# Perceiver layer on one core: P times V per head on four column groups, the mask added by TensorE, minima of two score banks at a time

## What is computed

```python
qh = split_heads(layernorm(x) @ Wq + bq)             # (64, 16, 32, 32)
kh, vh = split_heads(ctx @ Wk + bk), split_heads(ctx @ Wv + bv)   # (64, 16, 257, 32)
logits = einsum('bhqd,bhkd->bhqk', qh, kh) / sqrt(32)
logits = logits + mask * -1e9                        # mask: one row of 257 per sequence
attn = softmax(logits)
out = einsum('bhqk,bhkd->bhqd', attn, vh)
x = x + out.transpose(...).reshape(...) @ Wo + bo
```

## Time and profile before

| | us |
|---|---|
| median of 3 runs | 2039.79 |
| lowest and highest of them | 2039.04, 2040.78 |
| the profiled execution | 2034.94 |
| its span, first to last instruction | 2033.2 |
| TensorE matmul busy in it | 1902.7 (94%) |
| TensorE weight load busy (overlaps) | 1350.1 (66%) |
| VectorE busy | 1851.3 (91%) |
| ScalarE busy | 1682.3 (83%) |
| GpSimd busy | 494.9 (24%) |
| mean granted TensorE clock, share of full | 0.981 |

### The profile page before, as it was taken

How to read it: one execution, slowest core, us unless ns; L and a number is a source line. 1 busy time by engine, 2 the same in 40 slices (tenths; PEclk the granted TensorE clock), 3 DMA queues, 4 the chain that set the end, 5 groups by cost and what they waited for, 6 DMA issues and landing times. The chain is left out here.

```text
span 2033.2 us, 37605 instructions
## 1 busy us (share of the span) xinstructions
PE 1902.7 (94%) x11661; PEld 1350.1 (66%) x11676; DVE 1851.3 (91%) x2320; ACT 1682.3 (83%) x4617; POOL 494.9 (24%) x392
## 2 busy tenths in 40 slices
PE   7998999999999999999999999999999999668799
PEld 5576776767676666767676767666676767466444
DVE  1546999999999999999999999999999999999788
ACT  3458989898989889898989898888989898867484
POOL 1001214131414223141314142422314131201013
PEclk9999999999999999999999999999999999788899
DMA  9522333333342333333333334233333333420214
GB/s 295 213 82 89 79 93 79 92 81 96 72 114 65 83 98 73 93 83 92 77 91 82 98 72 114 62 84 93 80 93 83 91 78 88 95 84 11 73 42 145
DMA packets 93396, 188.55 MB, mean 93 GB/s; under 512 B 18768, under 2 KB 39904, under 8 KB 88160
## 3 DMA queue, kind: packets, MB, share of 16 engines
q1 hardware_dynamic: 78448, 133.32, 20.9%
q0 software_dynamic: 14832, 54.01, 14.1%
HBM read 116.12 MB, written 17.18 MB: 66 GB/s over the span
## 5 line engine op out<-in xcount | busy, mean ns | idle before, releaser
L1443 ACT ACTIVATE dA<-dt,A_sb 128x124 f32<-128x124 f32 x2048 | 617.0, 391 | 11.3 <-DVE dt L1770 10.1
L1820 DVE TENSOR_TENSOR_SCAN hb<-dA,hb 128x2048 f32<-128x2048 f32 x118 | 522.4, 4427 | 8.1 <-ACT dA L1443 4.3
L992 PE MATMUL bank<-ctxT,wk_sb 128*128 128x256 f32 x2048 | 461.6, 383 | 13.4 <-ACT ctxT L1259 11.4
L1003 PE MATMUL bank<-wv_sb,ctxT 128*128 128x512 f32 x1024 | 465.2, 595 | 2.3 <-ACT ctxT L1259 2.3
L992 PEld LDWEIGHTS bank<-ctxT,wk_sb 128*128 128x128 f32 x2048 | 382.6, 191 | 77.2 <-ACT ctxT L1259 18.2
L1003 PEld LDWEIGHTS bank<-wv_sb,ctxT 128*128 128x128 f32 x1024 | 186.6, 191 | 188.6 <-issue 185.1
L1545 POOL DMA_DIRECT2D hb<-hb x103 | 93.3, 906 | 862.5 <-DVE hb L1826 846.6
L1815 DVE TENSOR_TENSOR hb<-u,BC 128x2048 f32<-128x2048 f32 x118 | 270.4, 2292 | 5.7 <-DVE u L1782 2.6
L1826 DVE TENSOR_TENSOR hb<-hb,BC 128x2048 f32<-128x2048 f32 x117 | 268.2, 2292 | 1.5
L1096 PE MATMUL bank<-xn2T,win_sb 128*128 128x128 f32 x2048 | 236.8, 277 | 0.7 <-ACT xn2T L1358 0.7
L1096 PEld LDWEIGHTS bank<-xn2T,win_sb 128*128 128x128 f32 x2048 | 234.1, 193 | 4.5 <-issue 2.4
(11 more groups left out here) (167 smaller groups left out, 2582.2 us busy)
## 6 DMA issues: line engine op xcount, KB each, us to landing
hb<-hb POOLq DMA_DIRECT2D x103, 512.0 KB, 4.8
ctx_sb<-in_ctx_dram SPq DMA_DIRECT2D x64, 512.0 KB, 3.7
BC<-bcd_dram SPq DMA_DIRECT2D x32, 1024.0 KB, 7.0
maskb<-in_mask_Bx1x1xS_fk_dram SPq DMA_DIRECT2D x64, 128.5 KB, 3.4
wstage<-in_L_ffn_w_dram SPq DMA_DIRECT2D x4, 2048.0 KB, 11.7
x_sb<-in_x_dram SPq DMA_DIRECT2D x16, 256.0 KB, 3.5
win_sb<-in_L_attn_in_proj_w_dram SPq DMA_DIRECT2D x1, 4096.0 KB, 25.2
bo_sb<-bias_dram SPq DMA_DIRECT2D x64, 64.0 KB, 2.1
```

Of the source, the lines that this page charges most:

```text
L992: last = pe.matmul(bank[6 + j][:, (m % 2) * KF:(m % 2 + 1) * KF], wk_sb[:, c, m * P:(m + 1) * P], ctxT[:, c, :], start=(c == 0), stop=(c = ...
L1003: last = pe.matmul(bank[h][:], ctxT[:, c, h * P:(h + 1) * P], wv_sb[:, c, :], start=(c == 0), stop=(c == DC - 1))
L1443: last = act.activation(dA[:, c % 2, n * BT:(n + 1) * BT, 1:], dt[:, c, :].rearrange("p (b s) -> p b s", s=S)[:, :, 1:], ACT.Exp, scale=A_ ...
L1820: ins = dve.tensor_tensor_scan(flat, dA[:, c % 2].rearrange("p n s -> p (n s)"), flat, 0.0, ALU.mult, ALU.add)
```

## The change

Banks 2 to 5 become one tensor `score_banks` with four parts, so that an operation can read two neighbours; `bank[2]` to `bank[5]` still name the parts. Then:

- TensorE's `scores` begins with four products of one row each: a stationary row of 128 ones (`consts[row, 1:2]`, row 32 m) against `maskn[row, :]` of 257 columns opens the sum in bank `2 + m` over all 128 partitions, and the 16 score products add to it. TensorE now waits for `mask_scaled`; VectorE no longer does.
- VectorE's four passes become two `tensor_reduce` with min, each over two banks (2 by 257 elements to 2), which write the minima only. They no longer wait for the transposes of the sequence before, since `Pr` isn't written.
- ScalarE's exponentials read the banks in place of `Pr`.
- TensorE's `weigh_values` does each head by itself: 32 products (4 m, 2 halves h, 4 j) of 128 rows, 32 stationary columns and 32 moving columns, head slot j on column group j of the array, into a block of 128 partitions by 128 columns of bank 4 that has no unused part.
- ScalarE picks it up with one copy in place of four.
- What waited for the passes (`scored`) to free the banks waits for the exponentials (`exp_done`); GpSimd's `kv_keys` waits for the score products (`qk_psum`).

```diff
@@ scores, TensorE
-                    wait(pe, o_copied, HC * g)
+                    wait(pe, o_copied, g)
                     if b == 2 and to is not None:
                         pe.wait_ge(x2_ready, to + 1)
+                    pe.wait_ge(mask_scaled, g + 1)
                     apart(pe)
+                    for m in range(DC):
+                        row = slice(m * DEPTH, m * DEPTH + 1)
+                        pe.matmul(bank[2 + m][:, 0:KEYS], consts[row, 1:2].broadcast_to([1, P]), maskn[row, :],
+                                  start=True, stop=False)
                     for j in range(HC):
                         for m in range(DC):
                             rows = slice(m * DEPTH, (m + 1) * DEPTH)
                             last = pe.matmul(bank[2 + m][j * S:(j + 1) * S, 0:KEYS], Q[rows, j, b * S:(b + 1) * S],
-                                             KT[rows, j, 0:KEYS], start=True, stop=True)
+                                             KT[rows, j, 0:KEYS], start=False, stop=True)
@@ weigh_values, TensorE
                     for m in range(DC):
                         for h in range(2):
-                            last = pe.matmul(bank[4][:, m * P:(m + 1) * P], V[:, h, m * P:(m + 1) * P],
-                                             PT[:, h, m, :], start=(h == 0), stop=(h == 1))
+                            for j in range(HC):
+                                dims = slice(m * P + j * DEPTH, m * P + (j + 1) * DEPTH)
+                                last = pe.matmul(bank[4][j * DEPTH:(j + 1) * DEPTH, m * S:(m + 1) * S],
+                                                 V[:, h, dims], PT[:, h, m, j * S:(j + 1) * S],
+                                                 start=(h == 0), stop=(h == 1))
@@ mamba_turn, TensorE
-                    wait(pe, scored, keys - DC)
+                    wait(pe, exp_done, keys - DC)
@@ softmax, ScalarE
-                        act.wait_ge(scored, DC * g + m + 1)
-                        act.activation(Pr[:, m, :], Pr[:, m, :], ACT.Exp, scale=-1.0, bias=soft[:, 0, m:m + 1],
+                        act.wait_ge(scored, 2 * g + m // 2 + 1)
+                        act.activation(Pr[:, m, :], bank[2 + m][:, 0:KEYS], ACT.Exp, scale=-1.0, bias=soft[:, 0, m:m + 1],
@@ weigh_values, ScalarE
-                    for j in range(HC):
-                        rows = slice(j * DEPTH, (j + 1) * DEPTH)
-                        act.copy(oT[rows, :, b * S:(b + 1) * S],
-                                 bank[4][rows, :].rearrange("p (m q) -> p m q", m=DC)[:, :, j * S:(j + 1) * S]
-                                 ).then_inc(o_copied, 1)
+                    act.copy(oT[:, :, b * S:(b + 1) * S],
+                             bank[4][:, 0:DC * S].rearrange("p (m q) -> p m q", m=DC)).then_inc(o_copied, 1)
@@ kv_keys, GpSimd
-                    wait(pool, scored, DC * g)
+                    wait(pool, qk_psum, DC * g)
@@ scores, VectorE
-                    wait(dve, pt_psum, 2 * g)
-                    dve.wait_ge(mask_scaled, g + 1)
-                    apart(dve)
-                    for m in range(DC):
-                        self.score_pass(g, m)
+                    for m in (0, 2):
+                        dve.wait_ge(qk_psum, DC * g + m + 2)
+                        dve.tensor_reduce(soft[:, 0, m:m + 2], score_banks[:, m:m + 2, 0:KEYS], AX.X, ALU.min
+                                          ).then_inc(scored, 1)
```

More of the change, by code:

```diff
@@ L29 @@
 LOWEST = -3.0e38
-HIGHEST = 3.0e38
 def wait(engine, semaphore, value):
@@ L56, in sem, with psum @@
             return ctx.enter_context(nc.semaphore(name))
-        bank = [ctx.enter_context(nc.psum_tensor(f"bank{i}", [P, 512], F32)) for i in range(8)]
+        def psum(name, shape):
+            return ctx.enter_context(nc.psum_tensor(name, shape, F32))
+        bank = [psum("bank0", [P, 512]), psum("bank1", [P, 512])]
+        score_banks = psum("score_banks", [P, DC, 512])
+        bank += [score_banks[:, m, :] for m in range(DC)]
+        bank += [psum("bank6", [P, 512]), psum("bank7", [P, 512])]
         def keep(name, shape, dt=F32):
@@ L961, in last_values @@
                 def last_values(self):
-                    pe.wait_ge(scored, DC)
+                    pe.wait_ge(exp_done, DC)
                     for m in range(DC):
@@ L1013, in scores @@
                         pe.wait_ge(kcol_ready, 1)
+                        pe.wait_ge(setup_pool, 3)
                     if isinstance(g, int) and g == 1:
@@ L1054, in wo_product @@
                 def wo_product(self, t, keys):
-                    pe.wait_ge(o_copied, HC * BT * (t + 1))
+                    pe.wait_ge(o_copied, BT * (t + 1))
                     wait(pe, k_copied, keys)
@@ L1239, in _ @@
         def _(act):
-            act.wait_ge(setup_pool, 2)
+            act.wait_ge(setup_pool, 3)
             class Functions(Part):
@@ L1490, in _ @@
             pool.memset(dA[:], 0.0).then_inc(setup_pool, 1)
+            pool.memset(consts[:, 1:2], 1.0).then_inc(setup_pool, 1)
             pool.wait_ge(setup_pool, 1)
@@ L1692, in last_values @@
                                       bqkv[:, 2, :].unsqueeze(2).broadcast_to([P, DC, B]), ALU.add).then_inc(last_vT_ready, 1)
-                def score_pass(self, g, m):
-                    dve.wait_ge(qk_psum, DC * g + m + 1)
-                    apart(dve)
-                    dve.tensor_tensor_reduce(Pr[:, m, :], bank[2 + m][:, 0:KEYS], maskn[:], 1.0, HIGHEST,
-                                             ALU.add, ALU.min, soft[:, 0, m:m + 1]).then_inc(scored, 1)
-                def scores(self, g, t, b, to):
-                    wait(dve, pt_psum, 2 * g)
-                    dve.wait_ge(mask_scaled, g + 1)
-                    apart(dve)
-                    for m in range(DC):
-                        self.score_pass(g, m)
+                def scores(self, g, t, b, to):
+                    for m in (0, 2):
+                        dve.wait_ge(qk_psum, DC * g + m + 2)
+                        dve.tensor_reduce(soft[:, 0, m:m + 2], score_banks[:, m:m + 2, 0:KEYS], AX.X, ALU.min
+                                          ).then_inc(scored, 1)
                 def softmax(self, g):
```

## The result

| | before | after |
|---|---|---|
| median, beside one another on the same chip, us | 2039.41 | 2067.60 |
| lowest and highest | 2037.44, 2040.78 | 2066.07, 2069.44 |
| span of the profiled execution | 2033.2 | 2064.3 |
| mean granted TensorE clock in it | 0.981 | 0.967 |

The ratio is 1.0139, 95% interval 1.0122 to 1.0157: **slower by 28 us**. The forecast was 13.8 us faster, and the range ended at 2044.

The account below looks back on a forecast made before the run. VectorE's queue was taken to bound the interval, TensorE close behind. 14 intervals at -0.7 us (-9.8) and early savings of -2.4 and -1.6 make -13.8 us: 2026.0 us against 2039.79, range 2010 to 2044.

Parts of the forecast that it names:

- Waits added: TensorE's new wait for the mask is covered by 12 us; banks freed by the exponentials instead of the passes cost nothing.
- I price the clock at nothing: TensorE's granted clock was 1.00 in all three windows; its idle time would grow some 2 us of 110, at no cost.
- Rival B: Slower, TensorE takes the lead: P times V or mask passes don't overlap; 2059 to 2065 us, chance 0.16.
- P times V: On TensorE, per sequence: 64 passes of 32 columns on four column groups side by side take 0.8 us, for 1.79.
- Mask: On TensorE, per sequence: eight mask passes in four row groups side by side, with a tile shape change, add 0.65 us.
- Reduces: On VectorE, per sequence: two reduces take 1.24 us in place of 1.39 for four passes, -0.15 us.
- One copy: On ScalarE, per sequence: one 128 by 128 copy from a bank takes 0.28 us, for 1.09 in four, -0.8 us.
- Rival C: No change: on VectorE a reduce is no cheaper than two passes; 2036 to 2041 us, chance 0.14.
- x: Net change of TensorE's time per sequence from P times V and mask products: -0.34 us, between -0.69 and +2.0.
- The sum of -13.8 us: Whole kernel: -9.8 us over 14 intervals; before 233 us, -2.4 from TensorE and -1.6 from an earlier copy of V.
- VectorE's queue sets the interval: VectorE practically never stands still: over 14 intervals it waited 9.2 us for the exponentials and 0.8 us for the scores.
- of the 0.68 us wait a little: 0.1: VectorE's 0.68 us wait for ScalarE's exponentials in sequence 0 shrinks by 0.1 us an interval, as ScalarE comes earlier.

Follow-up runs that it names:

- after_unrolled: The changed kernel with TensorE's loop over tiles 3 to 14 written out, against the kernel before: 2019.04 us, ratio 0.9918.
- pv_unrolled: Kernel before with only P times V on column groups and its one copy, TensorE's loop written out: 2018.49 us, ratio 0.9905.
- mask_only: Kernel before with only the mask products, reduces and exponentials from the banks; P times V and four copies kept: 2057.16 us, ratio 1.0109.
- run 6: Kernel before with only P times V on column groups, loop kept, oT still copied by four copies: 2027.77 us, ratio 0.9955.
- pv_four_copies: The kernel of run 6: P times V on column groups alone, four copies of oT, against the kernel before: 2027.77 us.
- pad_160: Kernel before with one TensorE semaphore count, which nobody waits for, behind each key, value and Mamba input product: 2034.93 us, ratio 0.9988.
- pad_480: Kernel before with three TensorE semaphore counts, which nobody waits for, behind each key, value and Mamba input product: 2325.57 us, ratio 1.1413.

## Why the prediction was wrong, step by step

- **The step that failed** is the two sentences "*Waits added.* TensorE now waits for the mask ... nothing" and "I price the clock at nothing", read together: the list of what the change adds had the passes and the semaphores, and not the code. The change adds 450 instruction records to TensorE's loop, a third more, and takes it from 7 pieces to 9. That is 44.5 us in the eleven intervals behind a jump (1246.1 against 1201.6 in after_unrolled), out of the 48.4 between the two spans. The clock was in it as a consequence: without the stop it is at 1.00 from 450 to 1665 us. No rival had this; B was slower by another way, and that its 2059 to 2065 comes near the measured 2067.6 is chance.
- *P times V* at 0.8 us: 0.70. *Mask* 0.65: 0.65. *Reduces* 1.24: 1.21. *One copy* 0.28: about 0.3. Rival C is out by its own sign, the reduce being cheaper than two passes (0.61 us for 0.70); what it stood for, that taking this work from VectorE gives nothing in the whole, came all the same once the code was out of the way (pv_unrolled against after_unrolled).
- *Rival B* needed x above 0. It isn't (-0.44), but its mechanism is real: mask_only has x = +0.65 and lost 20 us (22 by the ratio). For the 14 intervals I had worked out 14 to 20 at that x, and they hold 16; of the 5 to 6 early the intervals of tiles 0 and 1 show 0.7. The 25 ns between starts by which B would have come, and which the Trainium skill gives as the least (TensorE: Matmul & The Clock Gate, the section on the 56 ns gap), don't hold across the column groups: 64 passes start 11 ns apart.
- *The sum of -13.8 us* comes near what the change brings where the code is no trouble: after_unrolled is 18 us below the kernel before. That is partly luck, for its shares are others. In the eleven intervals of tiles 4 to 14 I had put 0.6 each, 6.6 us, for VectorE's reduces and 0.1 each, 1.1 us, for ScalarE. With the loop written out P times V and its one copy give 6.7 (1212.9 to 1206.2 in pv_unrolled), most of it by the copies if run 6 holds there too, and the mask's half a further 4.6 (to 1201.6), which it loses again outside the loop. So "VectorE's queue sets the interval" held and "of the 0.68 us wait a little: 0.1" was the term mis-sized, with 0.5 us an interval by run 6: an engine that VectorE waits for once in each interval was worth more than the operations taken from VectorE. Of "the early part", forecast at 4.0 us, 2.8 came in the interval of tile 1 (104.1 for 106.9). That of tile 0 can't be told: 3.5 shorter in after_unrolled (89.8 for 93.3), 0.3 longer in the changed kernel (93.6), whose code is the same there.
- *The mask isn't late*: TensorE shows no wait for it in the loop.

What stays open: why the intervals of tile 1 and of the last tile are 1.8 and 1.4 us longer with the mask's half (TensorE's 0.65 us more in a sequence would do it, but no run tried it), why writing out the loop costs the kernel before 6 us, and what exactly makes a loop at the very start of its eighth piece tip.

## What to carry to other kernels

Count the instructions that a change adds inside a loop, on the engine where it adds them, as a cost of its own. Look in the page's queue list for code that is read: 33 packets before and 146 after is where this story shows. The count alone doesn't tell, for after_unrolled has 119 and pv_four_copies 130, and both are faster than before: look whether the engine stops on `issue` behind the jump. If a loop is over that edge, write it out, or move its start, so that the piece behind the jump lasts until the next has come, or until the engine has issued what the others wait for.

A product that wastes three quarters of its result can be split over the four column groups at less than half of its time, and what makes it pay may be the copy behind it rather than the product.

## What the runs showed of the hardware

- 64 float32 passes of 32 columns, spread over four column groups of TensorE, take 0.70 us, 11 ns from start to start (after).
- TensorE kept a loop that touched up to 7 pieces of 256 instructions (16 KB each) and read it in no turn (before, mask_only, pad_160); one that went well into an eighth was read in each turn, with one packet more than it has pieces. The jump then took 3.4 to 5.4 us for 0.3, the next piece came some 3.8 us later (after), and the engine stood still for up to 3.4 us; in the turn shown its granted clock was then 0.50, the 1.2 GHz level, for 6.7 us.
- Counting a semaphore isn't always free on TensorE: three counts behind each large product made an interval some 16 us longer (pad_480), one behind each cost nothing (pad_160).
